# Four engines in a new order where the first feed-forward layer gives way to attention

## What is computed

```
x = x + 0.5 * ffn(ln(x))      # experts: top 4 of 64, at most 32 rows each; and two shared ones
x = x + attention(ln(x))      # 16 heads of 128, weights = 4-bit codes * scales per 32 rows
x = x + 0.5 * ffn(ln(x))      # the same weights as the first
```

## Time and profile before

| | us |
|---|---|
| median of 3 runs (lowest, highest) | 967.13 (966.71, 968.01) |
| the profiled execution's own time | 967.17 |
| its span | 965.4 |
| PE busy in the span | 926.2 (96%) |
| DVE busy | 762.4 (79%) |
| ACT busy | 647.0 (67%) |
| POOL busy | 645.3 (67%) |

### The profile page before, as it was taken

The page is one execution under the profiler, slowest core; times in us unless marked ns, Lnnn a source line. Parts: engine busy times, 40 slices in busy tenths (PEclk is TensorE's granted clock), DMA queues, the critical chain, the costliest instruction groups (busy, mean ns, idle before and its releaser), DMA issues.

```text
span 965.4 us, 18681 instructions
## 1 busy us (share of the span) xinstructions
PE 926.2 (96%) x5851; PEld 560.8 (58%) x5859; DVE 762.4 (79%) x2083; ACT 647.0 (67%) x1426; POOL 645.3 (67%) x613
## 2 busy tenths in 40 slices
PE   7999889999999999999999999999999999988987
PEld 4766556555555555555555555555555555765666
DVE  7854399988888888888888888888878789875247
ACT  6534446887877787787778778777777777643431
POOL 3367779987576768778676766867677465326642
PEclk9999999999999999999999999999999999999999
DMA  8889745667666879798895766767675565385757
GB/s 344 350 267 310 274 155 164 109 132 121 137 142 105 164 147 191 154 204 175 169 188 98 158 109 130 153 99 144 107 155 90 97 112 96 71 330 175 255 209 272
DMA packets 302979, 165.60 MB, mean 172 GB/s; under 512 B 278176, under 2 KB 285600, under 8 KB 300832
## 3 DMA queue, kind: packets, MB, share of 16 engines
q1 hardware_dynamic: 297696, 146.56, 65.0%
q0 software_dynamic: 3072, 9.44, 2.9%
q10 hardware_dynamic: 2112, 8.39, 2.2%
HBM read 68.93 MB, written 28.31 MB: 101 GB/s over the span
## 4 chain that ended last, share of the span: by engine, by line
PE 76%; DVE 11%; DMA 4%; issue 3%; POOL 3%; ACT 2%; SPq 1%; DVEq 0%; POOLq 0%; ACTq 0%
PE b_o L110 5%; PE b_p L110 5%; PE b_o L111 5%; PE b_o L112 5%; PE b_p L112 5%; PE b_p L111 5%; PE b_s L111 5%; PE b_s L112 5%; PE b_s L110 5%; PE b_out L110 3%; PE b_out L112 3%; PE b_out L111 3%; PE b_v L110 2%; PE b_v L112 2%; PE b_v L111 2%
## 5 line engine op out<-in xcount | busy, mean ns | idle before, releaser
L2499 POOL TENSOR_TENSOR h<-pr,h 128x512 f16<-128x512 f32 x256 | 293.1, 1158 | 157.7 <-ACT h L1205 152.3
L1195 ACT ACTIVATE pr<-b_s,nmax,kappa 128x512 f32<-128x512 f32 x256 | 197.6, 774 | 38.3 <-DVE nmax L1953 35.2
L1950 DVE TENSOR_SCALAR_CACHE_REDUCE junk<-b_s 128x512 bf16<-128x512 f32 x256 | 174.9, 683 | 22.6 <-PE b_s L112 17.5
L1205 ACT ACTIVATE h<-pr 128x512 f16<-128x512 f32 x256 | 153.4, 626 | 3.5 <-DMA pT<-h 3.1
L1981 DVE SCALAR_TENSOR_TENSOR x<-b_out,rinv,x 128x256 f32<-128x256 f32 x256 | 111.3, 475 | 42.2 <-PE b_out L112 40.5
L110 PE MATMUL b_p<-xh,w 128*128 128x512 f16 x256 | 97.8, 382 | 2.8 <-DVE xh L1738 2.4
L110 PE MATMUL b_o<-pT,v 128*128 128x512 f16 x256 | 97.0, 379 | 1.7 <-DVE oT L1969 1.7
L112 PE MATMUL b_p<-xh,w 128*128 128x512 f16 x256 | 97.7, 382 | 0.0
L111 PE MATMUL b_p<-xh,w 128*128 128x512 f16 x256 | 97.6, 381 | 0.0
L110 PE MATMUL b_s<-kT,qT 128*128 128x512 f16 x256 | 97.0, 379 | 0.0
L111 PE MATMUL b_s<-kT,qT 128*128 128x512 f16 x256 | 97.0, 379 | 0.0
(11 more groups left out here) (230 smaller groups left out, 2240.9 us busy)
## 6 DMA issues: line engine op xcount, KB each, us to landing
raw<-in_experts SPq DMA_DIRECT2D x32, 768.0 KB, 7.7
raw_cs<-in_heads SPq DMA_DIRECT2D x16, 1024.0 KB, 5.0
zrows<-zero ACTq DMA_DIRECT2D x4, 2048.0 KB, 12.4
z<-zrows SPq DMA_DIRECT2D x16, 512.0 KB, 4.1
zrows<-zero SPq DMA_DIRECT2D x16, 512.0 KB, 4.2
zl<-zrows SPq DMA_DIRECT2D x16, 512.0 KB, 9.8
rows<-xn SPq DMA_DIRECT2D x8, 512.0 KB, 10.7
pT<-h SPq DMA_TRANSPOSE x256, 3.3
```

The source lines that it names most:

```text
L1195: act.activation(pr[n % 4][:], b_s[n % 3][:], ACT.Exp, bias=nmax[:, u % 2, i:i + 1], scale=kappa[:, s:s + 1], accum_out=rsum[:, u % 2, i:i ...
L1205: act.activation(h[n % 4][:, 0, :], pr[n % 4][:], ACT.Copy).then_inc(q["p_high"], 1)
L1950: dve.tensor_scalar(junk[n % 2][:], b_s[n % 3][:], 0.0, None, ALU.add, ALU.max, accum_out=peaks[:, n % 2:n % 2 + 1]).then_inc(q["peak_read ...
L2499: pool.tensor_tensor(h[n % 4][:, 1, :], pr[n % 4][:], h[n % 4][:, 0, :], ALU.subtract).then_inc(q["p_split"], 1)
```

## The change

Nothing is added. `warm_y(0, 8)` is removed from PE's list; all else is a new order of the same calls on DVE, ACT, POOL and SP, from `combine(3)` on.

```
@@ PE @@
             gate_up(13)
             down(2)
-            warm_y(0, 8)
             gate_up(14)
             turn(4)
@@ ACT @@
             normalise(4)
             hidden_high(12)
+            high(4)
             hidden_high(13)
-            high(4)
             silu(14)
-            squares_qk(1)
             silu(15)
             hidden_high(14)
+            keys_of(0)
             hidden_high(15)
-            keys_of(0)
             queries(0)
             queries(1)
             keys_of(1)
+            squares_qk(1)
             exps(0, 0)
             normalise(5)
@@ DVE @@
             combine(2)
+            hidden(13)
             combine(3)
             statistics(4)
-            hidden(13)
             shift(4)
             combine(4)
+            low(4)
+            add_shared(2)
+            hidden(14)
+            hidden(15)
+            keys_of(0)
+            queries(0)
             combine(5)
-            low(4)
-            hidden(14)
-            add_shared(2)
-            hidden(15)
             combine(6)
-            queries(0)
-            keys_of(0)
             combine(7)
             statistics(5)
             maxima(0, 0)
+            shift(5)
             maxima(0, 1)
             keys_of(1)
             queries(1)
-            shift(5)
             values(0)
@@ POOL @@
             hidden_low(10)
             hidden_low(11)
+            power(4)
             range_weights(0, 2)
             range_weights(0, 3)
             high_weights(0, 2)
             low_weights(0, 2)
+            hidden_low(12)
+            hidden_low(13)
             high_weights(0, 3)
             low_weights(0, 3)
-            power(4)
+            hidden_low(14)
+            hidden_low(15)
+            combine(8)
             scale_weights(1, 0)
             scale_weights(1, 1)
-            hidden_low(12)
-            hidden_low(13)
-            combine(8)
-            hidden_low(14)
-            hidden_low(15)
+            power(5)
             combine(9)
             combine(10)
-            power(5)
             combine(11)
-            combine(12)
             probs_low(0, 0)
             probs_low(0, 1)
+            combine(12)
             probs_low(0, 2)
             power(6)
@@ SP @@
             load_z(5)
-            load_qk(1)
             load_z(6)
             load_z(7)
             load_z(8)
+            load_qk(1)
             load_z(9)
```

## The result

The changed kernel takes 970.75 us (median of 6 runs, 970.30 to 972.69), against 967.73 us for the kernel before in the same runs: a ratio of 1.0026, 95% interval 1.0015 to 1.0037, or 1.5 to 3.6 us more. The profiled execution took 970.35 us, its span 968.5 us. Every ratio in this text is of undisturbed runs; the only other one is a run of e10 that took 2222.4 us.

What follows compares the result with a forecast made beforehand. POOL was taken to decide PE's exit from the ramp. 967.2 us plus 3.6 (power(6) 4.3 later, less 0.7 of slack) gave 970.8 us, range 965.0 to 973.5; slower by 1.9 to 4.9 us had chance 0.55.

Steps and rivals of the forecast that it cites:

- What bounds: From 260 us PE runs solid and hands a ramp shift on unchanged; POOL decides the exit from the ramp.
- Step 1: DVE ahead of the first tile of rows: combine(1) to (3) at 1.6 us each, shift(4) 2.7 us earlier.
- Step 2: PE up to the first keys: keys_of(0) near 134.5, 5 us earlier; removing the products of zeros costs nothing.
- Step 3: Second tile of rows: statistics(5) ends at 150.4, before 151.7; turn(5) comes at 153.8, 3.7 us earlier.
- Step 4: POOL: combine(9) and (10) now follow power(5), so power(6) comes at 168.8, 4.3 us later (bounds 1.8 to 5.6).
- Step 5: From POOL to PE: up to 0.7 us of POOL's delay is absorbed, leaving 3.6 us at 195.63.
- Step 6: SP: load_qk(1) lands near 143, POOL wants it at about 144; load_z(6) and (7) go out earlier.
- Faster: Rival: PE keeps the 3.7 us won at turn(5) because POOL's inputs have more slack: 963.5 us, chance 0.17.
- Absorbed: Rival: POOL's delay is mostly absorbed and PE loses 0 to 1.9 us: 968.1 us, chance 0.20.
- the second delay: Rival: late load_qk(1), slower combine or no saving on DVE puts POOL 7 us late at power(6): 974 us, chance 0.08.
- F: Theory stated for e9, not in the prediction: the first tile of rows decides, through PE; 1 us slower.

Runs made afterwards that it cites:

- e10: The changed kernel with SP's old order, load_qk(1) ahead of load_z(6) to (8): ratio 1.0048 to the kernel before, +4.6 us.
- e8: The kernel before with six additions on POOL behind power(5), which nothing reads (2.79 us): ratio 1.0008, +0.8 us.
- e5: The kernel before with one call moved, power(5) on POOL ahead of combine(9) and combine(10): ratio 1.0030, +2.9 us.
- e12: The kernel before with fourteen additions on POOL behind power(5), which nothing reads (6.6 us): ratio 1.0060, +5.8 us.
- e2: The kernel before with the new order on PE and DVE only, no products of zeros: ratio 1.0042, +4.1 us.
- e7: The changed kernel with range_weights(0, 2), (0, 3) ahead of power(4), combine(9), (10) ahead of power(5), combine(12) ahead of probs_low(0, 0): ratio 1.0033 to the kernel before.
- e11: The kernel before with POOL, SP and ACT of the change, but power(5) behind combine(9), (10) and combine(12) ahead of probs_low(0, 0): ratio 1.0029, +2.8 us.
- e1: The kernel before with the changed kernel's lists of POOL, SP and ACT, PE and DVE as before: ratio 1.0023, +2.2 us.
- e6: The kernel before without the eight products of zeros ahead of gate_up(14): ratio 0.9990, -1.0 us.
- e4: The changed kernel with power(5) back behind combine(9) and combine(10) on POOL: ratio 1.0036 to the kernel before, +3.5 us.
- e3: The changed kernel with one call moved, combine(9) on POOL ahead of power(5): ratio 0.9999 to the kernel before, -0.1 us.
- e9: The kernel before without the products of zeros and with add_shared(2) on DVE ahead of low(4): ratio 0.9991, -0.9 us.

## Why the prediction was right

**What bounds.** That the exit from the ramp follows POOL's `power(6)` held. Over the thirteen kernels of the table the ratio follows it to within 1 us, but for e8 (1.6); e5 and e12, which touch nothing but POOL, show it as a cause. That POOL alone sets it was said too strongly: in the kernel before, DVE's `veps` comes there level with POOL's work, and in e2, e7 and e11 POOL waits there for it. The forecast didn't suffer, since the change makes POOL later and that `veps` earlier. That a shift is handed on unchanged held once PE runs solid: from 222 us on the rows of PE are 2.7 us later, counted from `combine(0)`, as is `power(8)`, and the ratio gives 2.5.

**Step 1** held: three `combine` and `hidden(13)` in 5.5 us (5.4 forecast), `shift(4)` 2.7 us earlier (2.7). That POOL was the cause of the slow ones, which the rows of before couldn't show, is shown by e1, where DVE's list is the old one and `statistics(4)` comes at 124.32, 8.7 us behind `combine(0)` against 12.0.

**Step 2** held: `keys_of(0)` at +18.5 for 18.7 forecast, read from the twelve products of the first keys and queries, which start at 133.19. The products of zeros were worth nothing in time (e6).

**Step 3**: `turn(5)` came 3.5 us earlier (3.7 forecast). `veps` was 2.3 us earlier and not 1.3, as DVE is quicker while POOL idles (e5 shows the same); `low(5)` lost that again: 2.5 us behind `turn(5)` in place of 1.3. The half clock, of which I said that it costs nothing, has a part in this, and `maxima(0, 2)` ahead of it on DVE the rest. Where DVE stood idle for it (e11), `low(5)` was done 3.3 us behind the start of `turn(5)` in place of 2.6, so the half clock's part is some 0.7 us, an estimate from these two rows. In the changed kernel all of this lay under POOL's backlog; in e4, e7 and e11 it did not.

**Step 4** had the right terms and one size too large: 3.1 us later at `power(6)`, 4.3 forecast. 1.0 us of the difference is that of `veps`. The idle times were 8.31 us (8.3) and 3.01 us (1 to 3). That this is where the loss comes from is shown by e3: with one `combine` in the idle time it is gone.

**Step 5** took 0.7 us of slack and put the exit at 195.63. The profiles have 1.8 us left at `probs_values(2, 0)` (196.28, +81.6, before 195.63, +79.8), which is 1.3 of slack, and 2.7 us at `power(8)`, which is 0.4. Between the two, PE meets one more wait in the changed kernel (0.89 us ahead of 209.87, for a key plane from DVE), so the ramp ends later than I had put it. The whole shift was forecast as 3.6 us and is 2.5 by the ratio (1.5 to 3.6): 1.1 too large, by step 4, though the interval just reaches it. That the median is within 0.1 us of the forecast is luck, since the kernel before ran 0.6 us slower beside it than in the runs that the forecast started from.

**Step 6** held for the changed kernel (`load_qk(1)` at 135.27, POOL not waiting for it), but its sentence on the buffers was too short: e2 and e10 show that `load_z` in relation to `combine(5)` and `load_qk(1)` is worth 4.8 and 7.4 us of POOL's time.

**The rivals.** Faster, with PE keeping its 3.5 us, did not come, and its condition (POOL's delay under the slack) was not met, with POOL 3.1 us late at `power(6)`. In e3, where POOL is 0.8 us late and `turn(5)` 2.4 us earlier than before, nothing was gained either. *Absorbed* did not come, nor the second delay. What I didn't see as a rival, and what e4, e7 and e11 show, is that the second tile of rows can take the place of POOL's backlog at a like price. The chain of the kernel before had it: ahead of `power(6)` at 164.46 it runs through DVE and ACT, and I read it only from there on.

**Still open**: the size of POOL's slack (e8 against e12), whether the first tile of rows counts by a part of a us (F in e9), and why e6 should be 1 us faster than the kernel before.

## What to carry to other kernels

Before a wait is taken from the engine that is busiest, follow the chain past the ramp: here 5 us won on PE at the first keys were worth nothing, because POOL, 67% busy over the program, was the engine that the ramp waited for. An operation that is put ahead of others so that it is not late makes everything behind it wait when its input is later than the engine; put there just as much other work as fills the wait (one `combine` of 3.4 us in 3.0 us of idle time gave back 2.6 us). Look too at what the engine would wait for if its own work were done: in the kernel before the two were level, so more work moved ahead (e4, e7) only put the other in its place. Reordering a list moves the loads whose buffers it frees, so write down for each buffer who frees it and who wants it, as for e2 and e10.

## What the runs showed of the hardware

A sum of two tiles in SBUF on DVE (`combine`, three operations) takes 1.6 us while POOL idles and 2.7 us beside POOL's weight work. The Trainium skill (SBUF — State Buffer, SBUF: two separate sides) says that such a DVE instruction and a GpSimd instruction that reads SBUF exclude each other; the trace agrees, and shows that it can be used: a stretch in which POOL waits is one in which DVE is quick, so that part of POOL's idle time comes back: in e5 `veps` came 2.0 us earlier beside 3.98 us of it.

Behind a wait of PE of 4.97 us the granted clock was 0.50 from 153 to 157 us: eight transposes took 1.94 us in place of 1.09, a product 0.63 us in place of 0.38. Behind a wait of 3.40 us (e6, ahead of `gate_up(14)`) it was 0.50 from 130 to 134 us, and behind one of 2.40 us (the kernel before, ahead of the first keys) 0.51 from 140 to 143. Behind waits of 1.70 us (the kernel before) and 1.27 us (e8) the same transposes took 1.09 us. Eight products of zeros ahead of a wait of 2.06 us left it at 1.00 from 130 to 134 us; the half clock then fell on the first keys instead.
